# A mixer-plus-MLP block on one Trainium2 core: the first stage written in a new order on all five engines

## What is computed

```python
mod = (silu(c) @ wmod).reshape(4, 6, 1, 512)            # six "sections"
sa, ca, ga, sb, cb, gb = (mod[:, i] for i in range(6))  # ga, gb: sign kept, size at least 0.25
h = layernorm(x) * (1 + ca) + sa
x = x + ga * mixer(h)
h = layernorm(x) * (1 + cb) + sb
x = x + gb * (h @ binarized(weight).T + bias)

# mixer: 64 heads of 16, 8 groups with a state of 64, chunked scan
proj = h @ in_proj_w.T                                  # x, B, C (2048), z (1024), A_log (64)
xBC = silu(conv4_over_time(proj[..., :2048]) + bias)
dt = softplus(proj[..., 3072:])                         # a step size per token and head
y = ssd_scan(x, -dt, B, C) + D * x / dt
out = (y * silu(z + z_bias)) @ out_proj_w.T
```

## Time and profile before

| | us |
|---|---|
| median of 3 runs | 711.69 (711.49 to 714.23) |
| the profiled execution, its own time | 712.19 |
| its span, first to last instruction | 710.5 |
| first stage, up to the first projection of round -2 | 100.8 |
| first diagonal product (unit 0) | 119.1 |

### The profile page before, as it was taken

How to read it: one execution, slowest core, us unless ns; L and a number is a source line. 1 busy time by engine, 2 the same in 40 slices (tenths; PEclk the granted TensorE clock), 3 DMA queues, 4 the chain that set the end, 5 groups by cost and what they waited for, 6 DMA issues and landing times.

```text
span 710.5 us, 21292 instructions
## 1 busy us (share of the span) xinstructions
PE 654.0 (92%) x8347; PEld 494.7 (70%) x8347; DVE 521.6 (73%) x947; ACT 383.1 (54%) x834; POOL 358.5 (50%) x432
## 2 busy tenths in 40 slices
PE   5468787989999999999999999999998899999996
PEld 2254455767777777777777777777776667888884
DVE  3559839897787868768787777787779557687776
ACT  1664633545655554655554565555666526566655
POOL 7544401243653644456354374464646646756652
PEclk9678999999999999999999999999999999999999
DMA  9353301133322112132112233323211673344501
GB/s 261 89 209 88 109 32 59 61 92 108 97 66 78 57 66 92 50 123 85 36 65 91 71 107 115 97 86 104 81 50 67 183 239 118 119 128 136 153 36 68
DMA packets 61914, 70.52 MB, mean 99 GB/s; under 512 B 13972, under 2 KB 33460, under 8 KB 61816
## 3 DMA queue, kind: packets, MB, share of 16 engines
q1 hardware_dynamic: 56376, 69.12, 30.5%
q10 hardware_dynamic: 5440, 0.05, 0.5%
HBM read 54.45 MB, written 14.70 MB: 97 GB/s over the span
## 4 chain that ended last, share of the span: by engine, by line
PE 78%; DVE 6%; ACT 6%; issue 4%; POOL 3%; DMA 2%; SPq 1%; POOLq 0%; DVEq 0%; ACTq 0%
PE bank L1149 34%; PE bank L1899 11%; PE pair L1215 6%; PE bank L1158 4%; PE bank L1932 3%; PE pair L1203 3%; PE bank L739 3%; PE pair L1190 3%; PE pair L1228 2%; PE bank L1245 2%; DVE m_cv L1393 2%; PE pair L770 2%; PE bank L1167 2%; ACT p_hf L647 1%; DMA p_wm<-in_L_wmod_dram 1%
## 5 line engine op out<-in xcount | busy, mean ns | idle before, releaser
L1393 DVE SCALAR_TENSOR_TENSOR m_cv<-bank,gpc,m_cv 128x511 f32<-128x511 f32 (+2 forms) x192 | 143.4, 747 | 30.3 <-ACT m_cv L1304 25.6
L1149 PE MATMUL bank<-h_hi,w_hi 128*128 128x512 f32 x384 | 160.0, 417 | 4.8 <-ACT p_hf L647 1.7
L1149 PE MATMUL bank<-h_hi,w_lo 128*128 128x512 f32 x384 | 152.6, 397 | 0.0
L1149 PE MATMUL bank<-h_lo,w_hi 128*128 128x512 f32 x384 | 152.3, 397 | 0.0
L1528 POOL TENSOR_TENSOR m_S<-m_S,m_cd 128x128 f32<-128x128 f32 x96 | 39.7, 413 | 158.5 <-DVE m_S L1456 79.3
L1304 ACT ACTIVATE m_cv<-bank,gpc 128x512 f32<-128x512 f32 x96 | 71.8, 748 | 74.6 <-PE bank L1149 74.6
L1149 PEld LDWEIGHTS bank<-h_hi,w_hi 128*128 128x128 f32 x384 | 73.6, 192 | 20.7 <-issue 7.1
L1149 PEld LDWEIGHTS bank<-h_hi,w_lo 128*128 128x128 f32 x384 | 73.1, 190 | 17.0
L1149 PEld LDWEIGHTS bank<-h_lo,w_hi 128*128 128x128 f32 x384 | 73.7, 192 | 13.6
L1518 POOL TENSOR_TENSOR m_Xw<-m_Xp,wend 128x256 f32<-128x256 f32 x64 | 39.8, 621 | 85.3 <-ACT m_Xp L1324 85.3
L1316 ACT ACTIVATE m_M<-bank 128x512 f32<-128x512 f32 x128 | 76.2, 595 | 12.1 <-PE bank L1158 10.1
(11 more groups left out here) (174 smaller groups left out, 1275.2 us busy)
## 6 DMA issues: line engine op xcount, KB each, us to landing
m_ea<-ea_scratch SPq DMA_DIRECT2D x32, 256.0 KB
m_dd<-dd_scratch SPq DMA_DIRECT2D x32, 256.0 KB
y_scratch<-m_t SPq DMA_DIRECT2D x16, 512.0 KB, 3.3
h_lo_place<-y_scratch SPq DMA_DIRECT2D x16, 512.0 KB, 4.6
p_wm<-in_L_wmod_dram SPq DMA_DIRECT2D x6, 1024.0 KB, 7.0
m_wraw<-in_L_attn_in_proj_w_dram SPq DMA_DIRECT2D x18, 256.0 KB, 3.0
p_xt<-in_L_attn_input__dram SPq DMA_DIRECT2D x16, 256.0 KB, 3.8
w_lo_place<-in_L_attn_input__dram SPq DMA_DIRECT2D x16, 256.0 KB, 4.6
```

Of the source, the lines that this page charges most:

```text
L1149: ins = pe.matmul(A[k % 3][:, :], w[:, t, kc, :], h[:, n % NB, kc, :], start=(m == 0), stop=(m == 11))
L1393: ins = dve.scalar_tensor_tensor(out=cv[:, k % 3, lag:], in0=A[k % 3][:, 0:L - lag], scalar=s.gpc[:, gp, o:o + 1], in1=cv[:, k % 3, lag:], ...
```

## The change

No arithmetic of the result changes but the order of one sum; what each engine's queue holds, and in which order, does.

1. **Sections.** Each section was one accumulated product with 4 columns of weights: four matmuls one after the other on the same 4 rows of a bank. Now `scT` is padded to 32 columns, and the four matmuls write four strips of 32 partitions of a bank (`row_bank(n)[32k:32k+32]`), each started and stopped by itself. `copy_row` copies 128 x 512 in place of 4 x 512, and `turn_section` multiplies the row by a matrix `pick`, which adds the four strips. Sections 2 to 5 all use bank 7, each waits until the one before was copied.
2. **Batch by batch.** The first eight h blocks were made in one go, with all DVE and POOL odd and even low parts. Now ACT makes 0 to 3, turns four weight halves, makes 4 to 7, and four more weight halves. POOL makes all low parts but 5 and 7, which DVE does. `dt_inputs` is split by batch: 12 matmuls for batch 0 after its low parts, then weights, then 12 for batch 1. Roots are taken for 2 or 4 token tiles at once. Statistics have a slot per tile. The x tiles 4 to 7 and 12 to 15 go to buffers of their own (the `chain` of pair 1), so they are loaded without waiting.
3. **Fills and loads.** Six fills move from POOL to DVE, ahead of its first work. The copies of the constants into `R` and `Lm` move on ACT from after weights 3 to the very start, behind POOL's constant shapes. The 12 small loads move from ACT's queue to SP's, behind x tiles 0 to 7, two `w_mod` loads, `wa_raw` and two weight tiles; `wa_raw` goes behind the two `w_mod` loads.
4. **First stage's tail.** All 12 weight halves are turned before x tiles 8 to 15 are. `decays(0)` and `copy_row(4)`, `(5)` go before h 12 to 15 on ACT. PE runs `project(3)` and the turn of the decays, and goes to round -2.
5. **Into the rounds.** `turn_sections` and `gate_sizes` at round -2 slot 2, `dt_inputs(1, 1)`, `gate_turn` and `gate_rows` (with `softplus_inputs(1)`) at round -1 slot 0. On DVE: `mlp_columns` and `gate_values` in round -2, `softplus(1)` at (-1, 3), `skips(0)` at (0, 1), `finish_times(1)` at (0, 3), `sums(1)` at (1, 3), `low_sums(1)` at (2, 3), `skips(1)` at (4, 3). `decays(1)` moves from round 1 to 2, SP's `store_decays(1)` from 2 to 3, `store_skips(0)` from -1 to 0.

```diff
         def section(n):
             pe.wait_ge(d_wm[n % 2], 16 * (n // 2 + 1))
             if n == 2:
-                pe.wait_ge(w_act, 8)
-            if n == 4:
-                pe.wait_ge(h_act, 16)
+                pe.wait_ge(w_act, 10)
+            if n >= 3:
+                pe.wait_ge(sec_cp, n)
             for k in range(KC):
-                ins = pe.matmul(row_bank(n)[0:NB, :], scT[:, k, :], wm[:, n % 2, k, :], start=(k == 0), stop=(k == KC - 1))
+                ins = pe.matmul(row_bank(n)[32 * k:32 * k + 32, :], scT[:, k, :], wm[:, n % 2, k, :], start=True, stop=True)
             ins.then_inc(sec_pe, 1)
...
+    def dt_inputs(pe, pb, q):
+        wait_low(pe, 4 * (2 * pb + q) + 3)
+        if (pb, q) == (1, 0):
+            pe.wait_ge(sec_cp, 6)
+        first = 64 - 64 * q
+        for k in range(KC):
+            for n, (wt, h) in enumerate(((wa_hi, s.h_hi), (wa_hi, s.h_lo), (wa_lo, s.h_hi))):
...
+        weights(0)
+        weights(1)
+        turn(4)
+        turn(5)
+        weights(2)
+        weights(3)
+        turn(6)
+        turn(7)
+        dt_inputs(pe, 0, 0)
+        weights(4)
+        weights(5)
+        weights(6)
+        weights(7)
+        dt_inputs(pe, 0, 1)
+        project(0, 0)
+        project(0, 1)
+        weights(8)
+        weights(9)
+        weights(10)
+        weights(11)
+        for i in range(8, 12):
+            turn(i)
+        section(2)
+        project(1, 0)
+        project(1, 1)
+        section(3)
+        project(2, 0)
+        project(2, 1)
+        section(4)
+        section(5)
+        for i in range(12, 16):
+            turn(i)
+        dt_inputs(pe, 1, 0)
+        project(3, 0)
+        project(3, 1)
+        pe.wait_ge(h_act, 14)
+        end_turn(pe, 0)
...
+                    if (v, sl) == (-2, 2):
+                        start.turn_sections(pe)
+                    if (v, sl) == (-1, 0):
+                        start.dt_inputs(pe, 1, 1)
+                        start.gate_turn(pe)
...
                     if (v, sl) == (-1, 3):
+                        start.softplus(dve, 1)
+                    if (v, sl) == (0, 3):
+                        start.finish_times(dve, 1)
+                    if (v, sl) == (1, 3):
                         start.sums(dve, 1)
-                    if (v, sl) == (1, 3):
+                    if (v, sl) == (2, 3):
                         start.low_sums(dve, 1)
-                    if (v, sl) == (3, 3):
-                        start.skips(dve, 1)
+                    if (v, sl) in ((0, 1), (4, 3)):
+                        start.skips(dve, v // 4)
```

518 lines of the change are left out of this document (264 added, 254 removed).

## The result

The changed kernel takes 704.39 us (median of 5 runs, 703.48 to 706.49) against 711.69 (710.89 to 714.23). The ratio is 0.9892, with a 95% interval of 0.9871 to 0.9913: 1.1% faster, where 694 had been forecast. 704.39 lies just outside the range of 687 to 704, and the gain is 7.3 us instead of 18. The profiled execution has a span of 702.7 us (710.5 before).

A forecast was written before the change was run, and what follows sets the result against it. The first stage was taken as a relay without single bound, the rounds as TensorE's pace. First state copy 29.0 us earlier, 9 given back, 20.1 left, less 1.8 for contention: 18.3 off 712.2, forecast 694 (688 to 698; wider range 687 to 704).

The forecast's parts named there:

- To the first h block: Start of the first stage, through sections 0 and 1: h starts at 17.8 us, 4.0 earlier.
- The price of a section: Four matmuls in four column strips on TensorE: 1.3 us per section, between 0.9 and 1.6.
- Rival (a): Sections' four matmuls run in a row after all, 3.5 us each: 9.3 us later, 703; chance 0.09.
- the fills that I costed at nothing: Fills moved to DVE, 3.0 us, beside the load of section 0: no cost, even if delaying the condition 1.5 us.
- To the first step chain: First stage, low parts and step matmuls, POOL setting the pace: chain starts at 42 us, 6.5 earlier.
- The chain: First step chain on DVE: 14.6 us as before, ending at 56.6; 1.8 taken off the total gain for POOL contention.
- To the first state copy: From the chain's end through decays, row copies, section 5 and round -2: state copy at 83.7 us, 29.0 earlier.
- What the rounds give back: DVE's put-off work in the rounds, 36.4 us to unit 3's mix: 9 of the 29 us given back.
- the second `skips`: Put-off work that unit 6 pays as unit 5 did before; unit 6's diagonal at 144.0 us.
- One sign: In rounds 0 to 2 TensorE idles some 11 us in all, released by DVE or ACT behind it.
- (b): POOL and DVE slow each other throughout: before step inputs 3.4 us, chain 2.7, rounds' `silu` waits; 699 to 704, chance 0.17.
- (d): TensorE stays at the half clock between 18 and 84 us: 25 us later, 718; chance 0.03.

The follow-up runs named there:

- e4: Changed kernel with each section again one product accumulated over its four matmuls in 4 rows, with copies and transposes of 4 rows; ratio 0.9883 to the kernel before.
- e1: Changed kernel with VectorE's low part 7 moved directly behind low part 5, ahead of two normalized tiles and two statistics; ratio 0.9795 to the kernel before.
- e10: Changed kernel with e5 and e2 together, gate transpose and gate-row copy moved earlier, and two more moves in batch 1's order; 692.04 us, ratio 0.9679.
- e6: Changed kernel with GpSimd waiting for the end of the first step chain before weight halves 8 to 11 and low parts 8 to 15; 712.1 us, one run.
- e2: Changed kernel with ScalarE's row copies 4 and 5 ahead of the first decays, VectorE's tiles 12 to 15 normalized before the sums' low part; ratio 0.9828.
- e8: Changed kernel with the second step chain's ten polynomial steps cut to one column of 512, leaving out that computation; ratio 0.9838 to the kernel before.
- e5: Changed kernel with batch 1 reordered on GpSimd and VectorE: roots and statistics 4 to 7 earlier, low parts 1 and 3 on VectorE too; ratio 0.9763.
- e12: e10 with each section again one product accumulated in 4 rows, as in e4; ratio 0.9789 to the kernel before.

## Why the prediction was wrong, and where it was right

The sum failed at two steps, the one to the first step chain above all and the one to the first state copy; two others were right. By the prediction's own steps:

**To the first h block: 17.8 forecast, 19.44 measured.** The price of a section was right at full clock (1.3 put in, 1.06 measured), but section 0 ran at the half clock (1.94), which the sum had not. Rival (a), sections in a row, is refuted by the rows and by e4. Three more terms were too small. The loads land 0.9 and 0.5 us earlier than before (at 10.6 and 14.0), not up to 2, and section 1 now stands behind `wa_raw`, which lands at 14.75 (issue at 4.09 and 10.66 later); so section 0 ends at 12.6 and not at 10.9, section 1 at 16.4 and not at 14.7. Two `turn_section` take 1.85 us, not 1.4. And the fills that I costed at nothing do hold GpSimd's shapes up (to 10.3, forecast 8.8), which the loads then cover.

**To the first step chain: 42 forecast, 48.96 measured. This is the step that failed**, by 5.3 us beside the 1.6 carried in. GpSimd's queue was laid out nearly right: its low parts take 1.26 us there, and the fourth is done 12.7 us behind h block 0, where 11.6 had been laid out (its terms add up to 11.3). What failed is VectorE's queue, and the waits between the two. Low part 7 was to be done at 36.8 and was done at 42.45, 4.0 later than the 1.6 explain. It stands behind six statistics and low part 5, not four statistics. The eight normalized tiles 4 to 11 take 9.0 us, where at 0.56 each, their price alone, it would be 4.5; they run in part beside GpSimd's work. And VectorE waits 3.0, 1.1 and 1.5 us for roots and GpSimd 2.4 for a statistic, where one wait of 1.4 stood in the sum. The other 1.3 us are the step matmuls behind it, at the half clock after TensorE's 4.9 us of rest. e1 gets 3.5 us back by moving this one operation (4.3 counted from h block 0), e10 5.5 (chain at 43.41 though h block 0 was 1.3 later).

**The chain: 14.6, with 1.8 taken off for contention, so 16.4; measured 16.5.** The mechanism was right, and e6 gives its whole size: alone the chain takes 10.9, so 5.6 us of it are contention, of which the 14.6 of the kernel before had 3.7.

**To the first state copy: 27.1 behind the chain forecast, 31.6 measured.** This is the second step that failed, by 4.5 us. The decays, row copies and section 5 behind one another were in my sum, but the turns of tiles 12 to 15 behind section 5 were not: TensorE came out of a rest of 5.8 us and did section and turns at the half clock, 1.94 and 3.3 us. And the four `turn_section` in round -2, 3.5 us of TensorE's own time, stood in no term, and neither did the half clock behind them, some 1.5: this step of the sum called the round short of work and ended it with the last projection. e2 takes 3.1 of the 4.5 back.

**What the rounds give back: right in size.** 36.4 us of VectorE's list were forecast from the first state copy to unit 3's mix, and the distance to unit 3's diagonal is 36.7, as forecast (83.7 to 120.4). Of the 15.6 us at the first state copy 8.0 are left at unit 6, so 7.7 given back (forecast 9 of 29); the difference is the second `skips`, which costs unit 6 0.8 us over TensorE's pace where 2.2 were put in. e8 shows that the list is the cause. One sign was off: TensorE rests 6.6 us between the state copy and unit 3's diagonal, not some 11, and for a part of that time it has the half clock (granted 0.91). Since e1, e2, e5 and e10 keep that distance (36.3 to 36.6), each us won ahead of the first state copy arrives in full at unit 3.

Added up: 1.6, 5.3, 1.9 in the chain and 4.5, less 1.3 in the rounds, are the 12.2 us by which unit 6 is behind its forecast (156.17 and 144.0). 1.8 of them the forecast had taken off; 10.4 are left, and the result is 704.4 in place of 694.

**The rivals.** (b), GpSimd and VectorE slowing each other, priced at 699 to 704 with a chance of 0.17, names the right engines, and the result lies just beyond its far end. But none of its three terms came. Ahead of the step inputs GpSimd's low parts take 1.26 to 1.36 us (1.66 in (b)) and its weight halves 0.71 to 0.89 (1.03). The chain takes the 16.5 of the forecast, not 2.7 more. And the rounds give back no more than forecast. What was slowed there are VectorE's normalized tiles, which are in no term of (b); that its number is near is luck. Nor is the slowing the whole: with it still there, e10 is 13 to 14.5 us faster than the changed kernel (span and median). It costs little where TensorE doesn't wait behind it; the order of the queues decided where it would. Two engines that slow each other and also wait for each other are late by both. (d), the half clock up to 80 us, did not come as a whole, but in parts: 0.72 granted from 20 to 50 us and 0.89 from 50 to 97.

Two slips of the prediction change nothing: cold step matmuls end its second step at 43.6, not 43.8, and ACT's weight copies are 7.1 us in two waits, the longer of them 5.8.

What stays open: why e1's ratio is better than its marks by some 0.004, what exactly holds the loads of `w_mod` at 14 us (nothing here tried another order of loads), and what it would bring to avoid the half clock behind the section turns (nothing here tried another way to add the strips).

## What to carry to other kernels

In a stage that is a relay, the value of a shorter operation is decided by what waits beside it: the four strips cut each section by 2.5 us and brought 0 to 2 us in all, and 5 once the queues around them were in order. So look first at operations whose input is long there while another engine waits for their output; moving one line by four places brought 3.5 us, half of what the whole rewriting had brought (7.3). When two engines that slow each other also feed each other, lay out both queues with the contended durations and with the waits for each other. And put every instruction of a moved helper in the sum, also where the round that it goes to is called idle, and look at the clock behind it.

## What the runs showed of the hardware

- Four products in four column strips run at once: 8 records of 512 columns in 1.06 us at full clock, 3.60 in a row, 3.4 times as fast. Between them and the full-array products before and after no gap over 0.1 us shows.
- VectorE and GpSimd: `scalar_tensor_tensor` of 512 columns takes 0.69 to 0.72 us alone and 1.65 to 1.67 beside a low part of GpSimd (1.1 beside a weight half), `tensor_tensor` 0.69 and 1.65, the normalizing `tensor_scalar` 0.56 and up to 1.47, statistics 0.66 and 0.66.
- A rest can cost TensorE twice, and its length alone does not say whether. After 4.9 us without work the first seven step matmuls ran at 0.63 to 0.77 us, and after 4.1 us all twelve at 0.63 to 0.77 (e5); after 1.8 us they ran at 0.40 in e1, where TensorE had worked up to the rest, and all twelve at 0.63 to 0.77 in e10, where it had worked 1.06 of the 3.7 us ahead of them.
- Busy is not enough to keep the clock. The four section turns keep TensorE busy for 3.5 us with products of 4 columns, and in all eleven profiles that have them products of 512 columns behind them run at 0.63. In e4 and e12, whose turns are 1.1 us of transposes, they run at 0.40. So of the 10 us that the strips save on sections 2 to 5, the turns and the clock behind them take back 3.3.
- GpSimd's power of 4 columns took 1.05 us, of 2 columns 0.71: the price of a merged root is not that of one root.
